# A state-space and attention layer on one core: units of matmuls in half rows, three to three rounds

## The chip, the cores and the metric

One core of a Trainium2 chip runs the whole program as one launch. Its engines are TensorE (matrix products, into the PSUM memory), VectorE, ScalarE, GpSimd and SyncE (which issues DMAs). Each follows its own list of instructions in order, and they wait for one another through semaphores. The metric is the device time of a run in microseconds (us); lower is better.

## The reference

The input is x of 8 sequences x 512 tokens x 256 channels, in fp32. It is layer-normalised to xn, and three results are added to x:

```
u = conv1d(xn @ W_in + b_in, 4 taps, one filter for each of 512 channels) + conv_b
h = tanh(A) h + u_t * Bp ;  ys = Cp . h + Dp * u_t          (a scan over tokens, state of 16)
x += silu(ys) @ W_out + b_out
q, k, v = xn @ W_qkv + b_qkv                                 (16 heads of 16)
x += softmax(q k^T / 4) v                                    (512 x 512 for each head)
gate = softmax(xn @ W_gate + b_gate); the two largest kept as combine weights
x += sum over 8 experts of combine_e * (xn @ W_e + b_e)
```

## The kernel before

**Tiling.** A batch is one sequence: 512 tokens, four blocks of 128 rows. Most products need near-fp32 accuracy and are made of three: an operand is split into a rounded high part and the rest, and high x high, low x high and high x low are accumulated in one PSUM bank (`three`, L460). A *unit* is such a group with a bank of its own. Its kinds: T transposes xn (2 a batch), V makes values and gate logits (4), Q makes queries and keys (4), Z is the scan as a product with a Toeplitz matrix of its response (2), Y is the input projection on Z's result (4), M is half a pair of experts for one token block (16), O is the output projection (4), C transposes the combine weights (1), X transposes the row maxima (4), P transposes attention results (4), B and D belong to the start. M, Q and Y are 6 matmuls of 128 rows x 512 columns. Units share three PSUM banks, `FB`.

**Rounds.** The program is written as rounds t = 0, 1, ... (STEPS = 256, plus LAG = 11 and a few). Attention runs on pairs of heads of a group of four. In a round TensorE first does `score(t)` (L581): two matmuls of 48 rows each, one on rows 0 to 47, one on rows 64 to 111, into the two banks of `SB`. VectorE takes the row maxima of SB (`largest`, L1044), and the next score waits for it (`s_mx`). Then comes `turned(t - LAG)` (L595), the transposed scores less the maximum, again two matmuls of 50 rows, into the two banks of `TB`. ScalarE's exp (L827) turns TB into Pt, and the next turned score waits for that exp (`s_ex`). In every fourth round `values` (L612) multiplies 2 x 2 tiles of Pt with V, in four column groups, into `OB`. After these come the units of the round.

**Planner.** `plan` (L53) decides at build time in which round each unit goes. It spends TensorE time evenly by a table of costs (COST), knows of VectorE's load (VECTOR), takes units in the order of WANTED (32 b plus an offset in rounds) once `soonest` allows, and puts none in a round with values. A unit is read by ScalarE, and where it has a low part by VectorE, in its own round (`late`, all but the last unit) or at the start of the next (`early`, the last one). Reading M is two scaled copies into `mt`, a ring of NM = 4 buffers, and GpSimd adds each to `acc` (`grow`, L1114). The conv of Y is four taps on VectorE (`conv`, L884), one in each of the four rounds after the reading; then ScalarE's tanh, VectorE's gating product (L1082), ScalarE's high part yh and GpSimd's low part yl.

**Other queues.** SyncE copies query and key rows into the stacks `qst` and `kst` (rings of three groups, 12 DMAs a group, `half_stack`, L420) five rounds before a group's first score, once the turned scores that read the ring's old group are done, and the maxima's rows (`max_row`, L1260) after each X.

## Time and profile before

| | us |
|---|---|
| runs shown, median (lowest, highest) | 787.6 (786.55, 788.08) |
| span of the profiled execution | 784.0 |
| TensorE busy | 756.4 |
| VectorE busy | 582.2 |
| ScalarE busy | 534.5 |
| GpSimd busy | 389.7 |

The page gives the span, from the first to the last instruction of the execution that was profiled, as that execution's time; the runs of the table are others, without the profiler. Busy is the time in which an engine had at least one instruction in work. Matmuls are pipelined and the ends of their records are modelled, so that records overlap, and one has to look at the distances between their starts. The granted TensorE clock is full from the second slice of the span on.

### The profile page before, as it was taken

To read this page: it belongs to the slowest core of one execution; us is meant where nothing else is said; L and a number is where in the kernel's file an instruction comes from. 1 tells how busy PE (TensorE), PEld (TensorE's weight loads), DVE (VectorE), ACT (ScalarE), POOL (GpSimd) and SP (SyncE) were. 2 spreads that over 40 slices of the span, in tenths; PEclk is the share of its full clock that TensorE was granted. 3 is DMA by queue.
4 is the path that set the end of the run, shared out by engine and by line. 5 is a ranking of instruction groups with operands and counts; after the bars stand their busy time and mean duration, and the time that the engine had idled before them with its cause. 6 is when DMAs were issued, how large, how long until landed. Compare 5 with 4: busy or idle time off the path is not lost.

```text
span 784.0 us, 13236 instructions
## 1 busy us (share of the span) xinstructions
PE 756.4 (96%) x4408; PEld 455.7 (58%) x4408; DVE 582.2 (74%) x846; ACT 534.5 (68%) x926; POOL 389.7 (50%) x522
## 2 busy tenths in 40 slices
PE   9889999999999999999999999989999999999996
PEld 7566656566555665556555565556655565555553
DVE  6679785977679765897759877698767987568920
ACT  5546775676666766777667776667666776767775
POOL 8347482456344834455346373445444473435654
PEclk9979999999999999999999999999999999999999
DMA  8302111122110221102111121103111111112000
GB/s 272 68 8 66 46 24 30 30 69 69 35 29 22 69 69 41 42 15 82 42 42 42 42 86 32 39 23 96 42 42 43 42 49 41 46 39 69 22 2 27
DMA packets 32465, 39.09 MB, mean 50 GB/s; under 512 B 8513, under 2 KB 18535, under 8 KB 32398
## 3 DMA queue, kind: packets, MB, share of 16 engines
q1 hardware_dynamic: 31418, 37.29, 18.1%
q10 hardware_dynamic: 980, 0.96, 0.6%
q8 instruction: 35, 0.57, 0.3%
q14 instruction: 32, 0.26, 0.1%
HBM read 8.74 MB, written 4.19 MB: 17 GB/s over the span
## 4 chain that ended last, share of the span: by engine, by line
PE 80%; DVE 13%; issue 3%; POOL 2%; ACT 2%; DMA 0%; ACTq 0%; DVEq 0%; POOLq 0%
PE PS L464 38%; PE PS L624 13%; PE SB L591 12%; PE TB L608 7%; PE PS L521 4%; DVE mx L1049 4%; DVE xn L1026 2%; DVE ys L900 2%; PE PS L480 2%; DVE qkl L926 1%; POOL acc L1118 1%; PE PS L631 1%; DVE xl L932 1%; PE PS L476 1%; PE PS L555 1%
## 5 line engine op out<-in xcount | busy, mean ns | idle before, releaser
L1049 DVE TENSOR_REDUCE mx<-SB 128x2 f32<-128x1024 f32 x256 | 312.6, 1221 | 145.2 <-PE SB L591 144.3
L1118 POOL TENSOR_TENSOR acc<-acc,mt 128x256 f32<-128x256 f32 x320 | 252.7, 798 | 244.4 <-ACT mt L674 181.7
L827 ACT ACTIVATE Pt<-TB 128x1024 f32<-128x1024 f32 x251 | 257.5, 1026 | 58.1 <-PE TB L608 54.5
L674 ACT ACTIVATE mt<-PS,cpad 128x256 f32<-128x256 f32 x256 | 107.4, 470 | 58.5 <-PE PS L464 56.5
L591 PE MATMUL SB<-kst,qst 48*128 48x512 f32 x512 | 128.2, 497 | 12.1 <-DVE mx L1049 11.7
L624 PE MATMUL PS<-Pt,V 128*17 128x512 f32 x1024 | 122.3, 595 | 0.0
L591 PEld LDWEIGHTS SB<-kst,qst 48*128 48x128 f32 x512 | 47.8, 183 | 122.4 <-DVE mx L1049 70.3
L464 PE MATMUL PS<-weh,xTh 128*128 128x512 f32 x256 | 109.8, 429 | 1.9 <-DVE xTl L913 1.2
L608 PE MATMUL TB<-qst,kst 50*128 50x512 f32 x502 | 101.3, 399 | 1.3 <-ACT Pt L827 1.3
L464 PE MATMUL PS<-wel,xTh 128*128 128x512 f32 x256 | 100.9, 394 | 0.0
L464 PE MATMUL PS<-weh,xTl 128*128 128x512 f32 x256 | 100.7, 393 | 0.0
L900 DVE SCALAR_TENSOR_TENSOR ys<-uc,cwc,ys 128x511 f32<-128x511 f32 (+2 forms) x96 | 87.4, 910 | 0.0
L464 PEld LDWEIGHTS PS<-weh,xTh 128*128 128x128 f32 x256 | 48.4, 189 | 29.5 <-issue 15.3
L624 PEld LDWEIGHTS PS<-Pt,V 128*17 128x17 f32 x1024 | 23.5, 96 | 63.0 <-issue 62.6
L1243 POOL TENSOR_TENSOR yl<-th,yh 128x512 fp32r<-128x512 f32 x32 | 42.9, 1339 | 31.6 <-ACT yh L760 31.6
L464 PEld LDWEIGHTS PS<-wel,xTh 128*128 128x128 f32 x256 | 48.1, 188 | 11.1
L464 PEld LDWEIGHTS PS<-weh,xTl 128*128 128x128 f32 x256 | 48.4, 189 | 7.0
L608 PEld LDWEIGHTS TB<-qst,kst 50*128 50x128 f32 x502 | 47.7, 186 | 5.9 <-ACT Pt L827 5.5
L1127 POOL TENSOR_TENSOR acc<-acc,at 128x256 f32<-128x256 f32 x31 | 23.1, 747 | 55.4 <-DVE at L960 54.6
L464 PE MATMUL PS<-wouth,yh 128*128 128x256 f32 x128 | 37.3, 292 | 0.3 <-DVE xl L932 0.3
L464 PE MATMUL PS<-woutl,yh 128*128 128x256 f32 x128 | 35.9, 280 | 0.0
L464 PE MATMUL PS<-wouth,yl 128*128 128x256 f32 x128 | 35.9, 280 | 0.0
(162 smaller groups left out, 1138.9 us busy)
## 6 DMA issues: line engine op xcount, KB each, us to landing
qst<-qkh SPq DMA_DIRECT2D x124, 64.0 KB, 2.3
kst<-qkh SPq DMA_DIRECT2D x124, 64.0 KB, 2.3
out<-acc SPq DMA_DIRECT2D x8, 512.0 KB, 2.8
qst<-qkl SPq DMA_DIRECT2D x62, 64.0 KB, 2.2
kst<-qkl SPq DMA_DIRECT2D x62, 64.0 KB, 2.3
acc<-in_x SPq DMA_DIRECT2D x7, 512.0 KB, 3.9
Bt<-in_wexp SPq DMA_DIRECT2D x2, 512.0 KB, 8.0
raw<-in_wexp SPq DMA_DIRECT2D x2, 512.0 KB, 8.5
```

The costliest lines, as they stand in the source:

```text
L464: ins = e.matmul(P, u, v, start=(start and k == 0), stop=(stop and k == n - 1))
L521: ins = e.matmul(P[:, lo:lo + n], p[:, c, fs], q[:, r:r + n], start=(k == 0), stop=(k == 11))
L591: ins = e.matmul(SB[:, h, :], qst[rows, g % 3, jj, 128 * a:128 * a + 128], kst[rows, g % 3, jj, :], start=True, stop=True)
L608: ins = e.matmul(turned_bank(t)[:, h, :], kst[rows, g % 3, jj, 128 * a:128 * a + 128], qst[rows, g % 3, jj, :], start=True, stop=True)
L624: ins = e.matmul(OB[32 * j:32 * j + 17, :], V[:, g // 4 % 2, a, 4 * (g % 4) + j, :], Pt[:, (2 * m + j % 2) % NP, j // 2, :], start=(a == 0 ...
L674: return e.activation(mt[:, item % NM, :], P, ACT.Copy, scale=scale)
L827: e.activation(Pt[:, T % NP, :, :], turned_bank(T)[:, :, :], ACT.Exp, scale=0.25).then_inc(s_ex, 1)
L900: ins = e.scalar_tensor_tensor(out=y[:, s:512], in0=v[:, 0:512 - s], scalar=cwc[:, d, 3 - s:4 - s], in1=y[:, s:512], op0=ALU.mult, op1=ALU ...
L1049: e.tensor_reduce(mx[:, g % 2, 0:2, 4 * jj + a], SB[:, :, :], AX.X, ALU.max).then_inc(s_mx, 1)
L1118: e.tensor_tensor(v, v, mt[:, item % NM, :], ALU.add).then_inc(s_mt, 1)
L1127: e.tensor_tensor(v, v, at[:, :].rearrange("p (a c) -> p a c", a=4), ALU.add).then_inc(s_ad, 1)
L1243: e.tensor_tensor(yl[:, d, :], th[:, :], F(yh[:, d, :]), ALU.subtract).then_inc(s_yl, 1)
```

## The change

Rounds are grouped by four. The numbers of rows in a matmul, and where a unit goes, change as follows.

- LAG is 12, so that values fall in rounds with t % 4 = 0.
- M, Q and Y (24 a batch) go into rounds t % 4 = 1, 2, 3, in threes a, b, c. `side_by_side` does half of each of two units' products: 6 pairs of matmuls, one of the pair on rows 0 to 63 of its operands, the other on rows 64 to 127. The pairs are (a, c), (b, a), (c, b), so each unit has its lower rows in one round and its upper rows in another, accumulated in its bank.
- Rounds with t % 4 = 0 hold values, then X, P or up to two of T, C, V, which now use the halves of TB as banks 3 and 4 (after the exp of the same round; the next turned score waits until they are read), then one of Z, O, V, B at full height in one of the three banks. X is a matmul with the identity on 16 columns of maxima instead of a transpose of 72.
- Units a are read in round 3, b and c in the next round 0, the whole unit in the next round 1.
- The planner places each tap, gating product and high part of Y by VectorE's load (`room`), at most 2.3 us a round by its own figures, 3.2 where t % 4 = 0. VectorE does a second tap of a round and the gating after its unit readings. Layer norm goes one piece a round over eight rounds; the gate's steps are spread over eleven rounds (`GATE` has a second column of rounds).
- zh and zl get tensors of their own, and both matmuls of a score and of a turned score increment the semaphore. The two Z are read one by one.
- The first eight rounds hold up to two units each.

The products themselves are collected by a new generator, `products(u)`, which yields what `three` was called with before; a unit at full height goes through it in a loop (`in_one`).

```diff
-LAG = 11
+LAG = 12
 END = STEPS + LAG + 5
 FREE = STEPS - LAG + 1
 NP = 5
 NM = 4
+CYCLE = 8
...
+WANTED = {("T", i): -60 for i in range(2)}
 WANTED.update({("V", i): -30 for i in range(4)})
-WANTED.update({("Z", i): -20 for i in range(2)})
-WANTED.update({("Q", i): -30 for i in range(4)})
-WANTED.update({("Y", i): 4 * i - 8 for i in range(4)})
+WANTED.update({("Z", i): -52 for i in range(2)})
+WANTED.update({("Q", i): -30 + 8 * (i // 2) for i in range(4)})
+WANTED.update({("Y", i): 4 * i - 20 for i in range(4)})
-WANTED.update({("O", i): i // 2 * 8 + 6 + i % 2 * 2 for i in range(4)})
+WANTED.update({("O", i): i // 2 * 8 + i % 2 * 2 for i in range(4)})
...
+READ = {"T": 0.7, "V": 0.17, "Q": 0.75, "Z": 0.7, "P": 0.7, "X": 0.28}
+
+LN = {b: max(32 * b - 29, 0) for b in range(1, NB)}
...
+GATE_US = {"m": 0.2, "z": 0.2, "r": 0.2, "x0": 0.2, "q0": 0.4, "y0": 0.2, "k0": 0.45, "d": 0.2, "x1": 0.2, "q1": 0.4,
+           "y1": 0.2, "k1": 0.45, "l": 0.5}
...
+    vector = {t: 1.25 * (0 <= t < STEPS) for t in range(-2, END + 60)}
+    for g in range(NG):
+        vector[8 * g + 8] += READ["X"]
+        vector[8 * g + LAG + 12] += READ["P"]
+    for b in range(1, NB):
+        for k in range(4):
+            vector[LN[b] + k] += 0.6
+            vector[LN[b] + 5 + k] += 0.6
...
+    def most(t):
+
+        if t < 16:
+            return 2.6
+        return (3.2 if t % 4 == 0 else 2.3) - 1.0 * (t >= STEPS) * (t % 4 == 0)
+
+    def room(us, t):
+
+        while vector[t] + us > most(t):
+            t += 1
+        vector[t] += us
+        return t
...
+            first = max(r, taps[n - 1][3], gating[n - 2] + 1 if n >= 2 else 0) if n else max(r, 8)
+            taps[n] = []
+            for s in range(4):
+                first = room(0.93, first)
+                taps[n].append(first)
+            gating[n] = room(0.82, max(first + 2, yhi[n - 1] + 2 if n else 0))
+            yhi[n] = gating[n] + 1
...
+        elif t % 4 == 0:
+            room_tb = 2 if t % 8 == 4 or t > STEPS + LAG else 0
+            while room_tb:
+                u = take(lambda u: u[0] in "TCV" and soonest(*u) <= t and (u[0] != "T" or room_tb == 2 - u[2]))
+                if u is None:
+                    break
+                whole[t].append(u)
+                put(u, t, t)
+                room_tb -= 1
+            left = sum(u[0] in "QYM" for u in todo)
+            slots = 3 * ((STEPS + LAG - t) // 4)
+            u = take(lambda u: u[0] in "ZOVB" and soonest(*u) <= t)
+            if u is None and left > slots:
+                u = take(lambda u: u[0] == "M" and soonest(*u) <= t)
+            if u is not None:
+                whole[t].append(u)
+                put(u, t, t + 1)
+            if t < STEPS + LAG - 3:
+                three = []
+                for late in (1, 1, 2):
+                    u = take(lambda u: u[0] in "QYM" and soonest(*u) <= t + late
+                             and not (u[0] == "Y" and any(v[0] == "Y" for v in three)))
+                    if u is not None:
+                        three.append(u)
+                if len(three) == 3:
+                    a, c, b = three
+                    if c[0] == "Q" and a[0] != "Q":
+                        a, c = c, a
+                    sides[t + 1], sides[t + 2], sides[t + 3] = (a, c), (b, a), (c, b)
+                    for u, n in ((a, 1), (c, 1), (b, 2)):
+                        at[u] = t + n
+                    put(a, t + 2, t + 3)
+                    put(b, t + 3, t + 4)
+                    put(c, t + 3, t + 4)
...
+            if CYCLE <= t < STEPS + LAG and done[u] == read[u]:
+                give(u, (4 if u[0] == "P" or u[0] != "X" and n else 3,), t)
+            else:
+                give(u, range(3), t + n / 8)
+        for u in sides.get(t, ()):
+            if u not in unit:
+                give(u, range(3), done[u] + 0.9)
...
+TURNED_AFTER = {}
+for _u in UNIT.values():
+    if _u.bank > 2:
+        TURNED_AFTER.setdefault(max(_u.t + 1 - LAG, 0), []).append(_u)
...
+        FB = [P[:, :] for P in PS[1:4]] + [TB[:, h, :] for h in range(2)]
...
-                e.wait_ge(s_ST, 8 * (g - 2))
+                e.wait_ge(s_ST, 16 * (g - 2))
...
+            def side_by_side(low, up):
+
+                for u in (low, up):
+                    if u not in begun:
+                        bank_there(u)
+                        operands_there(u)
+                if low in begun:
+                    e.wait_ge(s_high, begun[low])
+                if up in begun:
+                    e.wait_ge(s_low, begun[up])
+                for k, ((o, v, w, _), (p, a, b, _)) in enumerate(zip(products(low), products(up))):
+                    below = e.matmul(o, v[0:64], w[0:64], start=(k == 0 and low not in begun), stop=(k == 5 and low in begun),
+                                     skip_group_check=True)
+                    above = e.matmul(p, a[64:128], b[64:128], start=(k == 0 and up not in begun),
+                                     stop=(k == 5 and up in begun), skip_group_check=True)
+                if low in begun:
+                    below.then_inc(s_full[low.bank], 1)
+                else:
+                    below.then_inc(s_low, 1)
+                    begun[low] = firsts[0] = firsts[0] + 1
+                if up in begun:
+                    above.then_inc(s_full[up.bank], 1)
+                else:
+                    above.then_inc(s_high, 1)
+                    begun[up] = firsts[1] = firsts[1] + 1
+
+            def bank_there(u):
+                if u.before is not None:
+                    e.wait_ge(*bank_read(u.before))
+                elif u.bank > 2:
+                    e.wait_ge(s_kp, 1)
+                    e.wait_ge(s_kv, 17)
+                if u.bank > 2 and u.t >= LAG:
+                    e.wait_ge(s_ex, u.t - LAG + 1)
...
+                for u in TURNED_AFTER.get(t, ()):
+                    e.wait_ge(*bank_read(u))
...
                 for h in range(2):
                     rows = slice(64 * h, 64 * h + 50)
-                    ins = e.matmul(turned_bank(t)[:, h, :], kst[rows, g % 3, jj, 128 * a:128 * a + 128], qst[rows, g % 3, jj, :],
-                                   start=True, stop=True)
-                ins.then_inc(s_ST, 1)
+                    e.matmul(turned_bank(t)[:, h, :], kst[rows, g % 3, jj, 128 * a:128 * a + 128], qst[rows, g % 3, jj, :],
+                             start=True, stop=True).then_inc(s_ST, 1)
 
...
                 for m in values_at(t):
                     values(m)
+                if t in SIDES:
+                    side_by_side(*SIDES[t])
                 for u in AT[t]:
                     unit(u)
...
-                for s in (3, 2, 1, 0):
-                    for b, d in y_read(t - s - 1):
-                        conv(b, d, s)
                 for u in early(t):
                     if u.kind != "D":
                         unit(u)
-                for b, d in y_read(t - 5):
-                    e.wait_ge(s_th, 4 * b + d + 1)
-                    e.scalar_tensor_tensor(out=th[:, :], in0=th[:, :], scalar=1.0, in1=ys[:, d % 2, :], op0=ALU.add,
-                                           op1=ALU.mult).then_inc(s_y, 1)
+                taps = taps_at(t)
+                for b, d, k in taps[0:1]:
+                    conv(b, d, k)
                 for b, name in gate_at(t, "DVE"):
                     gate(b, name)
                 for b in range(1, NB):
-                    if t - LN[b] in (0, 1):
-                        layer_norm(b, 2 * (t - LN[b]))
-                        layer_norm(b, 2 * (t - LN[b]) + 1)
-                    elif 3 <= t - LN[b] < 5:
-                        layer_norm(b, 2 * (t - LN[b]) - 1)
-                        layer_norm(b, 2 * (t - LN[b]))
+                    k = t - LN[b]
+                    if 0 <= k < 4 or 5 <= k < 9:
+                        layer_norm(b, k)
                 for u in late(t):
                     unit(u)
                     if t == -1 and (u.kind, u.i) == ("T", 1):
                         split(W_VG)
+                for b, d, k in taps[1:]:
+                    conv(b, d, k)
+                for b, d in gating_at(t):
+                    e.wait_ge(s_th, 4 * b + d + 1)
+                    e.scalar_tensor_tensor(out=th[:, :], in0=th[:, :], scalar=1.0, in1=ys[:, d % 2, :], op0=ALU.add,
+                                           op1=ALU.mult).then_inc(s_y, 1)
                 at_start(t)
```

## Rows read from the trace of the kernel before

**Rows 1.** The head of the page

```profile
span 784.0 us, 13236 instructions
```

**Rows 2.** A window over rounds 8 to 255; timeline rows of its outer scores

```profile
54.70:751.60 696.90, 683.08 (x4004) 406.95 (x4003) 540.84 (x760) 487.14 (x832) 343.92 (x455) 1.00 0.18 46
...
54.68 0.50 PE L591 MATMUL SB<-kst,qst 48*128 48x512 f32 x2
...
751.58 0.50 PE L591 MATMUL SB<-kst,qst 48*128 48x512 f32 x2
```

**Rows 3.** Timeline of TensorE: start, duration, engine, line, output<-input, count

```profile
402.32 0.40 PE L464 MATMUL PS<-weh,xTl 128*128 128x512 f32 x1
402.56 0.40 PE L464 MATMUL PS<-wel,xTh 128*128 128x512 f32 x1
402.89 0.50 PE L591 MATMUL SB<-kst,qst 48*128 48x512 f32 x2
403.22 0.40 PE L608 MATMUL TB<-qst,kst 50*128 50x512 f32 x2
403.55 0.50 PE L464 MATMUL PS<-xh,winh 128*128 128x512 f32 x1
403.89 0.40 PE L464 MATMUL PS<-xh,winl 128*128 128x512 f32 x1
```

**Rows 4.** The same stretch, timeline of TensorE's weight loads

```profile
402.89 0.19 PEld L591 LDWEIGHTS SB<-kst,qst 48*128 48x128 f32 x2 [0.37 <-issue]
402.99 0.19 PEld L608 LDWEIGHTS TB<-qst,kst 50*128 50x128 f32 x2
403.55 0.19 PEld L464 LDWEIGHTS PS<-xh,winh 128*128 128x128 f32 x1 [0.37 <-ACT mt L674]
403.66 0.19 PEld L464 LDWEIGHTS PS<-xh,winl 128*128 128x128 f32 x1
```

**Rows 5.** Timeline of TensorE in a round with values, and the score after it

```profile
405.80 1.91 PE L624 MATMUL PS<-Pt,V 128*17 128x512 f32 x16
407.64 0.50 PE L591 MATMUL SB<-kst,qst 48*128 48x512 f32 x2
```

**Rows 6.** Timeline of a round without a long unit

```profile
679.87 0.49 PE L591 MATMUL SB<-kst,qst 48*128 48x512 f32 x2
...
680.41 1.23 DVE L1049 TENSOR_REDUCE mx<-SB 128x2 f32<-128x1024 f32 x1 [1.01 <-PE SB L591]
...
681.69 0.50 PE L591 MATMUL SB<-kst,qst 48*128 48x512 f32 x2 [0.53 <-DVE mx L1049]
```

**Rows 7.** Timeline of VectorE

```profile
415.25 1.21 DVE L900 SCALAR_TENSOR_TENSOR ys<-uc,cwc,ys 128x510 f32<-128x510 f32 x1
416.38 1.21 DVE L1049 TENSOR_REDUCE mx<-SB 128x2 f32<-128x1024 f32 x1
417.52 0.73 DVE L900 SCALAR_TENSOR_TENSOR ys<-uc,cwc,ys 128x509 f32<-128x509 f32 x1
418.18 0.41 DVE L1013 BATCH_NORM_STATS2 st<-acc 128x6 f32<-128x256 f32 x1
```

**Rows 8.** Timeline of ScalarE

```profile
438.43 0.84 ACT L674 ACTIVATE mt<-PS,cpad 128x256 f32<-128x256 f32 x2
439.16 1.03 ACT L827 ACTIVATE Pt<-TB 128x1024 f32<-128x1024 f32 x1
```

**Rows 9.** Groups by shape, then the page's group of taps: count | busy, mean ns

```profile
L913 DVE TENSOR_TENSOR xTl<-PS,xTh 128x512 fp32r<-128x512 f32 x16 | 10.3, 675 | 0.0
...
L1118 POOL TENSOR_TENSOR acc<-acc,mt 128x256 f32<-128x256 f32 x320 | 252.7, 798 | 244.4 <-ACT mt L674 181.7 <-ACT mt L673 42.6 <-POOL acc L1118 0.4
...
L900 DVE SCALAR_TENSOR_TENSOR ys<-uc,cwc,ys 128x511 f32<-128x511 f32 (+2 forms) x96 | 87.4, 910 | 0.0
```

**Rows 10.** Timeline of SyncE: issues of a stack; the page: issue, us to landing

```profile
462.93 1.29 SPq L437 DMA_DIRECT2D qst<-qkh  x2
...
qst<-qkh SPq DMA_DIRECT2D x124, 64.0 KB, 2.3
```

More of the change, by code:

```diff
@@ new lines, in plan @@
+def plan():
+    whole = {t: [] for t in range(-2, END + 1)}
+    sides = {}
+    at, done, read = {}, {}, {}
+    taps, gating, yhi = {}, {}, {}
+    xh = {0: -1}
+    todo = sorted([(k, b, i) for b in range(NB) for k, i in WANTED if b == 0 or k != "B"],
+                  key=lambda u: 32 * u[1] + WANTED[u[0], u[2]])
+    vector = {t: 1.25 * (0 <= t < STEPS) for t in range(-2, END + 60)}
[15 more added lines that the diff above has]
+        return t
@@ L93, in soonest @@
+            return max(t, after(("B", 0, 3), 1) if b == 0 else after(("O", b - 1, i // 2 * 2 + 1), 0))
         if kind in "CM":
[L94 to L109 removed]
+            late = {name: g[2 if b == 0 else 3] for name, g in ((g[0], g) for g in GATE)}
@@ new lines, in take @@
+    def take(test):
+        k = next((k for k, u in enumerate(todo) if test(u)), None)
+        return None if k is None else todo.pop(k)
+    for t, row in FIRST.items():
+        for k, (kind, i) in enumerate(row):
+            u = (kind, 0, i)
+            if u in todo:
+                todo.remove(u)
+            whole[t].append(u)
+            put(u, t, t + (k == len(row) - 1))
+    for t in range(2, END):
+        g = normal_at(t)
+        if g is not None:
+            u = ("P", g // 4, g)
+            whole[t].append(u)
+            put(u, t, t)
@@ new lines, in plan @@
+        assert b == 0 or done["C", b - 1, 0] < done["V", b, 3] + 9
+        assert b < 2 or done["M", b - 2, 15] < done["V", b, 3] + 9
+        assert b == 0 or xh[b - 1] + 4 < LN[b] + 5 and done["T", b - 1, 1] < LN[b] + 5
+    order = sorted(done, key=lambda u: (read[u], done[u] == read[u]))
+    ends = {t: [] for t in whole}
+    for u in order:
+        ends[read[u]].append(u)
+    item = {u: 2 * n for n, u in enumerate(u for u in order if u[0] in "MO")}
+    uses, frees, held, busy = [0] * 5, [0] * 5, [None] * 5, [-9] * 5
@@ new lines, in plan, with give @@
+    unit = {}
+    def give(key, banks, n):
+        kind, b, i = key
+        bank = min(banks, key=lambda j: busy[j])
+        busy[bank] = n
+        uses[bank] += 1
+        frees[bank] += kind not in "MO"
+        unit[key] = Unit(kind, b, i, at[key], done[key], read[key], bank, uses[bank], frees[bank], item.get(key), held[bank])
+        held[bank] = unit[key]
+    for t, row in whole.items():
+        for n, u in enumerate(row):
+            if CYCLE <= t < STEPS + LAG and done[u] == read[u]:
[5 more added lines that the diff above has]
+                give(u, range(3), done[u] + 0.9)
@@ new lines, in plan @@
+    return ({t: [unit[u] for u in row] for t, row in whole.items()},
+            {t: [unit[u] for u in two] for t, two in sides.items()},
+            {t: [unit[u] for u in row] for t, row in ends.items()}, taps, gating, yhi, xh)
+AT, SIDES, READS, TAPS, GATING, YHI, XH = plan()
+UNIT = {(u.kind, u.b, u.i): u for row in READS.values() for u in row}
+TURNED_AFTER = {}
+for _u in UNIT.values():
+    if _u.bank > 2:
+        TURNED_AFTER.setdefault(max(_u.t + 1 - LAG, 0), []).append(_u)
+KRYLOV = {("T", 1): (1, 2), ("D", 0): (3,), ("D", 1): (4,), ("D", 2): (5,), ("D", 3): (6,)}
```

391 lines of the change are left out of this document (189 added, 202 removed), and 7 rows, old and new, of the table GATE.

## The prediction, made before the changed kernel ran

> **What bounds the kernel now.** The page gives a span of 784.0 us [rows 1]. The median of the runs shown is 787.6 us, 3.6 above that span; I make the sum on the span and carry the difference over. A window over the steady part, from the score of round 8 (54.68) to that of round 255 (751.58), has 247 rounds in 696.9 us [rows 2], so four rounds (a cycle, since the P V products come every fourth round) take 696.9 / 61.75 = 11.29 us. TensorE is busy 683.1 of it, VectorE 540.8, ScalarE 487.1, GpSimd 343.9.
>
> A "busy" TensorE says little by itself, so next comes its timeline, matmul by matmul [rows 3]. Inside an expert unit, matmuls of 512 columns start 0.23 apart. From the unit's last to the score it is 0.33, from score to turned score 0.33, from there to the next unit 0.33, and from that unit's first matmul to its second 0.34. The weight loads explain it [rows 4]: the score's load starts together with its matmul's record (402.89), not under the matmul before it, and so does the unit's (403.55); the turned score's two loads start at 402.99, under the score's stream, and its matmuls follow 0.23 later. So each change between half-height pairs (rows 0 to 63 beside 64 to 127) and full height costs about 0.10 of emptying and 0.10 of bare load, 0.21 in all. A round has two: 0.41.
>
> Both matmuls of a score or turned score start together and take one slot of 0.23 before the next starts. That is the evidence that two half-height matmuls run side by side at the price of one.
>
> **What the change removes.** Streamed columns stay the same: a unit of 6 full-height matmuls becomes 12 of half height, in pairs with another unit's. Three units in three rounds are 18 pairs x 0.23, as 18 full matmuls were. What goes is the change of mode. Before, a cycle has 8 changes (2 x 4; in the round with values, turned to values and values to score). After, rounds t%4 = 1, 2, 3 are half height throughout, and round 0 has three: turned to values, values to whole unit, whole unit to the next score. Five fewer x 0.21 = 1.03 us a cycle. TensorE's own need falls from 11.29 to 10.26.
>
> Cross-check from below: a paired round is 8 pairs x 0.232 = 1.86, three with one bare load 5.68 [rows 3, 4]. Round 0 is score and turned 0.56, values 1.84 [rows 5], on average 2.1 of whole units and transposes (per batch Z 4.0, O 6.4, V 3.2, T, C, P and X 3.3 from their column counts at 0.23 per 512) and 0.1 of emptying: 4.6. The sum is 10.28.
>
> **What it makes late next.** Now a paired round is so short that others can end last. Three waits appear.
>
> (a) VectorE's chain. Row by row in [rows 6]: a score recorded at 679.87 lets the row maximum start at 680.41 (0.54), which runs 1.23, and the next score comes at 681.69: 1.82 a round with nothing else on VectorE, just under 1.86. VectorE's records overlap: maximum to next instruction is 1.14, and a tap is followed after 0.66, or after 1.13 in its slow form (415.25) [rows 7]; mean duration 0.91 less 0.08 of overlap gives 0.83 a tap. The three paired rounds then last at least 0.54 + 1.14 + o1 + 1.14 + o2 + 1.23 + 0.05 = 4.10 + o1 + o2, where o1 and o2 is VectorE's other work of rounds 1 and 2 (that of round 3 falls into the long round 0). It costs when o1 + o2 is over 1.58. I walked the new planner through one batch of 32 rounds: it fills each paired round to its limit of 2.3 less 1.25, that is one tap a round (or layer norm at 0.55, a Q or Z split at 0.6 to 0.7, and what the planner's table GATE_US says of the gate). o1 + o2 comes to 1.93, 2.11, 1.68, 1.66, 2.26, 2.13, 0.7, 0 for the eight cycles, so 0.35 + 0.53 + 0.10 + 0.08 + 0.68 + 0.55 = 2.3 us a batch.
>
> (b) ScalarE in round 0. Units b and c of a trio both end in round 3 and are read in round 0 ahead of the exp: two M are four copies, 0.73 a pair, then exp at 1.03 [rows 8]. They start about 0.2 into the round, so the exp ends at 0.2 + 1.48 + 1.03 = 2.71. The transposes of round 0 now go to the halves of TB and wait for this exp; TensorE is there at 0.56 + 1.84 = 2.40. That is a stall of 0.36 when b and c are two M, less with a Q or Y, none where VectorE's chain delayed the round; with a tanh ahead 0.48. Over a batch I count 1.5 us.
>
> (c) The two T of a batch in TB (t = 12 of 32). The next turned score must wait until ScalarE has cast and VectorE has subtracted both (0.68 for each subtraction [rows 9]; 0.6 for each cast is an estimate from the exp of twice its columns [rows 8]), and this batch puts a tap behind them. T's are written from 2.73 to 3.6, subtractions end near 5.3, the tap at 6.0, so the next maximum starts 1.8 later than TensorE alone would allow: 1.8 us a batch.
>
> Together 5.6 us a batch, 0.70 a cycle. The last batch has no next one to prepare, about 0.2; averaged with it, 0.64. The waits of before that vanish are about 0.1 and I leave them.
>
> **Edits priced at nothing.** Zh and zl of their own only loosen a wait. Two Z in separate rounds, each read by itself, cost the same work. X as a plain matmul with 16 columns: still 0.06. The taps after the units' reads: the total is unchanged, its place is in (a). For the stacks of group g SP issues 12 DMAs at 0.65 (7.7 us) and the last lands 2.3 later, 10 us after the turned score of round 8g-5 has freed the ring [rows 10]; with LAG 12 instead of 11 this comes a round later, but round 3, a round 0 and three paired rounds are 1.9 + 4.0 + 5.7 = 11.6 at least, less 0.7 to the release. It fits by about 1 us; without that cover each us by which it is missed is paid once a group, 30 us over the kernel. More rows of SP (max rows, 4 issues) stand ahead of it, but are done in round 0. GpSimd adds each half M at 0.80 [rows 9]: 8 in a cycle of 11 are 6.4, plus yl and xl; its four mt buffers are freed in time unless it lags.
>
> LAG + 1 adds one round to the end, without a score: 1.1 to 2.0, taken as 1.5. The first eight rounds keep their work and their start-up waits, taken at 0 (bounds -3 to +3, one unit's worth of two matmul groups either way).
>
> One rule speaks against it: the page "TensorE: Matmul & The Clock Gate" of the Trainium skill (The cost: per-tile semaphore tail) gives about 26 ns for each further increment, and the change adds one to each score and turned score. By it some 30 ns would stand before each maximum and exp. No run here shows it yet; the sum without it stands.
>
> **The sum.** 11.29 - 1.03 + 0.64 = 10.90 us a cycle; x 61.75 this is 24 us less; + 1.5: 22.5 less, 765. Counted from below (65 us for rounds 8 to 31, six batches at 45.4 + 36.8 + 5.6 = 87.8, the last 78) the cycles take 670 us instead of 699.5, which gives 759.5. I take the middle, 762.
>
> **Rivals.**
> 1. *The waits hide.* The planner leaves VectorE's work where round 0 covers it, and neighbours' slack absorbs (b) and (c). Then only 1.03 x 61.75 = 63.6 is left of the terms: 725.5; with half the waits, 745. For it: a fifth of VectorE's time is free [rows 2]. Against: that slack sits in round 0.
> 2. *VectorE and ScalarE chain at full duration* (the other side). If the overlap of records is lost and more taps are slow, because GpSimd works beside them, the chain is 4.27 + o1 + o2 with taps at 0.91 and more: 4.6 us a batch for (a), 2.9 for (b) (four copies at 0.47), 2.0 for (c), 1.19 a cycle, 1.07 averaged: 11.33, +2.5 + 1.5 gives 792. It decides from 1.03 us of waits a cycle, 0.39 above mine. For it: tap means of 0.91 lie between 0.66 and 1.13 [rows 7, 9]. Against: the overlaps in rows 7 and 8.
> 3. *GpSimd's ring.* ScalarE's third and fourth copy in round 0 wait for an addition that a yl held up (over 1 us, an estimate from 0.80 for half its columns [rows 9]); each cycle with one loses 0.9 and the exp, hence the transposes, come late. Half the cycles: 0.45 x 61.75 = 28, 790. Against: GpSimd is idle half the time [rows 2].
> 4. *The pairs don't overlap in a long run.* Each load of a half would wait for the matmul of its own half: 18 bare loads x 0.107 = 1.9 us a cycle, 119 us, 881. Rows 3 and 4 speak against it: the turned score's loads start under the score's matmuls on the same rows. But they show one pair behind one pair, not 48 pairs in a row, and none that accumulates. The Trainium skill, page "TensorE: Matmul & The Clock Gate" (The mechanism), says that a load overlaps matmuls in flight only when the row group differs, which would be this rival; by the full-height loads of rows 4 the trace disagrees.
>
> **Chances.** Forecast (748 to 778) 0.51; rival 1, 0.17; rival 2, 0.17; rival 3, 0.10; rival 4, 0.05. What a measurement of this kernel can tell from no change is about 0.2%, 786.0 to 789.2. A quarter of rivals 2 and 3 still ends below that band, so faster is 0.51 + 0.17 + 0.06 = 0.74; of the rest 0.05 within it, 0.21 slower. Leaving out the lower half of rival 1 and the worst of 2 to 4, the range is 738 to 796; the likeliest case's own is 748 to 778.
>
> **What would show it.** In the changed trace, paired matmuls of two units starting together, a pair every 0.23, and no 0.33 step between turned score and the pairs (else rival 4). Cycles of 10.8 to 11.0 us. TensorE's waits for VectorE's maximum at the scores of rounds 2, 3 and 0 in cycles with taps; waits of the transposes for the exp of the same round, near 0.3; one long wait at t = 13 of each batch for xTl. ScalarE's copies waiting for GpSimd would be rival 3, taps near 1.2 throughout rival 2. Scores waiting for stack DMAs would show that the LAG sentence was wrong.

## The result and the profile after

| | before | after |
|---|---|---|
| runs, median (lowest, highest), us | 787.84 (786.55, 789.42) | 766.25 (764.93, 767.8) |
| ratio of the medians, 95% interval | | 0.9731 [0.9707, 0.9756] |
| span of the profiled execution | 784.0 | 764.9 |

The change makes the kernel 21.6 us faster; 762 was forecast, with 738 to 796 as its range. Head of the page after, with the first row of its busy times (busy, share of the span, instructions), to set beside [rows 1]:

```profile
span 764.9 us, 15809 instructions
...
PE 723.7 (95%) x5568; PEld 487.4 (64%) x5568; DVE 559.9 (73%) x845; ACT 531.8 (70%) x926; POOL 389.8 (51%) x522
```

The window from the score of round 8 to that of round 255, as in [rows 2]. Its ends are the starts of the two scores' weight loads, and so it is with all lengths of rounds and batches below; in the changed kernel a score's matmul starts 0.12 behind its load where pairs stand before it (round 255's at 732.11). The row gives (length; busy and instructions of TensorE, weight loads, VectorE, ScalarE, GpSimd; granted clock; DMA share; GB/s):

```profile
58.10:731.99 673.89, 654.93 (x5155) 441.87 (x5157) 515.63 (x759) 486.05 (x837) 347.16 (x457) 0.99 0.19 47
```

So these 247 rounds take 673.9 us, against 696.9, and a cycle 673.89 / 61.75 = 10.91 (10.90 was forecast). The start up to round 8 is 3.4 us longer (58.1 against 54.7) and the end after round 255 0.5 longer (764.9 - 732.0 against 784.0 - 751.6): -23.0 + 3.4 + 0.5 = -19.1, the difference of the spans.

**A paired round.** TensorE and its loads in round 138 from its score on (start, duration; a load's line is PEld). L765 is the score, L783 the turned score, L677 and L679 the lower and upper halves of a pair:

```profile
417.01 0.19 PEld L765 LDWEIGHTS SB<-kst,qst 48*128 48x128 f32 x2
417.13 0.41 PE L765 MATMUL SB<-kst,qst 48*128 48x512 f32 x2
...
417.36 0.41 PE L783 MATMUL TB<-qst,kst 50*128 50x512 f32 x2
...
417.60 0.40 PE L679 MATMUL PS<-xTh,wqkh 64*128 64x512 f32 x1
417.60 0.19 PEld L679 LDWEIGHTS PS<-xTh,wqkl 64*128 64x128 f32 x1
...
417.61 0.39 PE L677 MATMUL PS<-weh,xTh 64*128 64x512 f32 x1
417.61 0.19 PEld L677 LDWEIGHTS PS<-weh,xTl 64*128 64x128 f32 x1
...
417.84 0.39 PE L679 MATMUL PS<-xTh,wqkl 64*128 64x512 f32 x1
...
417.84 0.40 PE L677 MATMUL PS<-weh,xTl 64*128 64x512 f32 x1
...
418.07 0.39 PE L679 MATMUL PS<-xTl,wqkh 64*128 64x512 f32 x1
```

Score to turned score 0.23, to the first pair 0.24, pair to pair 0.24 and 0.23: the steps of 0.33 of [rows 3] are gone. Two things are to be seen. The halves of two units start together and take one slot. And the loads for the pair of 417.84 start at 417.60, with the matmuls of the pair before them on the same rows. A round without a wait lasts 1.85 to 1.86.

**Round 0.** TensorE and ScalarE in round 136, t = 8 of its batch, from the values (L798) on. L1004 is the exp, L711 is P, L706 is X, L663 the whole unit; L880 and L851 read the units that ended in round 3:

```profile
410.23 0.69 ACT L880 ACTIVATE qkh<-PS,bq 128x512 fp32r<-128x512 f32 x1 [0.38 <-PE PS L679]
...
410.64 1.91 PE L798 MATMUL PS<-Pt,V 128*17 128x512 f32 x16
410.82 0.83 ACT L851 ACTIVATE mt<-PS,cpad 128x256 f32<-128x256 f32 x2
...
411.54 1.03 ACT L1004 ACTIVATE Pt<-TB 128x1024 f32<-128x1024 f32 x1
...
412.67 0.63 PE L711 MATMUL TB<-ident,ot 128*128 128x128 f32 x4
413.22 0.11 PEld L706 LDWEIGHTS TB<-ident,mx 128*16 128x16 f32 x2 [0.17 <-issue]
413.22 0.39 PE L706 MATMUL TB<-ident,mx 128*16 128x128 f32 x2
...
413.54 0.19 PEld L663 LDWEIGHTS PS<-wouth,yh 128*128 128x128 f32 x1 [0.21 <-issue]
413.55 0.39 PE L663 MATMUL PS<-wouth,yh 128*128 128x256 f32 x1
```

Values take 1.84 [rows 5], so TensorE is free near 412.5; the exp ends at 412.57 and P starts at 412.67. That is term (b), small here: one of the two reads is a Q. From P's first matmul to the whole unit's it is 0.88, and two loads in it stand bare, before X and after it. What X and these two loads take is a cost that the forecast put at 0.06.

**Averages.** The distances between scores, averaged over the five batches 2 to 6 of every trace, give for the kernel after 87.6 us a batch (87.8 was counted): 41.9 in the eight rounds 0 and 45.7 in the 24 paired ones. The sums below compare with these.

**The wait at the T's, and that at t = 26.** VectorE and the score's load, first in round 141 (t = 13), then in rounds 153 to 155 (t = 25 to 27):

```profile
425.33 0.68 DVE L1090 TENSOR_TENSOR xTl<-TB,xTh 128x512 fp32r<-128x512 f32 x1
...
425.93 0.92 DVE L1077 SCALAR_TENSOR_TENSOR ys<-uc,cwc,ys 128x511 f32<-128x511 f32 x1
...
426.77 1.21 DVE L1222 TENSOR_REDUCE mx<-SB 128x2 f32<-128x1024 f32 x1
...
428.04 0.19 PEld L765 LDWEIGHTS SB<-kst,qst 48*128 48x128 f32 x2 [0.42 <-DVE mx L1222]
...
460.12 0.68 DVE L1107 TENSOR_TENSOR zl<-PS,zh 128x512 fp32r<-128x512 f32 x1
...
460.72 0.68 DVE L1266 SCALAR_TENSOR_TENSOR th<-th,ys 128x512 f32<-128x512 f32 x1
...
461.32 1.22 DVE L1222 TENSOR_REDUCE mx<-SB 128x2 f32<-128x1024 f32 x1
...
462.59 0.18 PEld L765 LDWEIGHTS SB<-kst,qst 48*128 48x128 f32 x2 [0.50 <-DVE mx L1222]
```

In the first, the tap behind the second T's subtraction makes the maximum late; the round lasts 2.17, that is 0.32 over a free one, not 1.8. In the second, round 25 has Z's subtraction and a gating product behind its maximum, 1.2 us together; the next score is 0.5 late. It is the largest single loss in a paired round.

**The start.** Round 4, VectorE, GpSimd and TensorE, and the same operation in the trace before:

```profile
36.77 2.34 POOL L1339 TENSOR_TENSOR wel<-Bt,weh 128x1024 fp32r<-128x1024 f32 x1
...
36.95 2.83 DVE L1205 TENSOR_TENSOR Rl<-ys,Rh 128x640 fp32r<-128x640 f32 x1
...
39.93 0.76 PE L663 MATMUL PS<-Rh,xh 128*128 128x512 f32 x1 [3.19 <-DVE Rl L1205]
```

```profile
35.77 0.79 DVE L1032 TENSOR_TENSOR Rl<-ys,Rh 128x640 fp32r<-128x640 f32 x1
...
36.62 2.37 POOL L1168 TENSOR_TENSOR wel<-Bt,weh 128x1024 fp32r<-128x1024 f32 x1
```

The first Z waits 3.2 us for an operation that took 0.79 in the trace before, where the wait was 0.6. In the kernel after it begins 0.18 behind a GpSimd subtraction and ends 0.67 behind that one's end; before, it was through when GpSimd began that subtraction (a short GpSimd product had begun 0.16 after it). All the runs below are like the kernel after in this (2.83 or 2.84, each begun 0.18 behind `wel`). No run moves one of the two alone, so that GpSimd's work is the cause is likely and not shown.

### The profile page after: what moved, and what is told of

The parts are those of the page before. It is cut to its first block, busy times and chain, and to the rows that moved or that the text cites. A ratio compares the mean times of both kernels' runs of the same rounds, so it can differ in the third digit from the quotient of the medians.

```text
span 764.9 us, 15809 instructions
## 1 busy us (share of the span) xinstructions
PE 723.7 (95%) x5568; PEld 487.4 (64%) x5568; DVE 559.9 (73%) x845; ACT 531.8 (70%) x926; POOL 389.8 (51%) x522
## 4 chain that ended last, share of the span: by engine, by line
PE 85%; DVE 7%; issue 4%; ACT 4%; DMA 1%; ACTq 0%; SPq 0%; POOL 0%; DVEq 0%; POOLq 0%
PE PS L677 20%; PE PS L798 14%; PE PS L663 13%; PE PS L679 12%; PE SB L765 9%; PE TB L783 7%; DVE mx L1222 3%; PE TB L711 3%; PE TB L663 2%; ACT Pt L1004 1%; PE TB L706 1%; PE PS L805 1%; ACT mt L851 1%; PE TB L718 1%; PE PS L584 1%
## 5 line engine op out<-in xcount | busy, mean ns | idle before, releaser
L1004 ACT ACTIVATE Pt<-TB 128x1024 f32<-128x1024 f32 x250 | 258.1, 1032 | 53.9 <-PE TB L783 49.7
L798 PE MATMUL PS<-Pt,V 128*17 128x512 f32 x1024 | 123.7, 601 | 0.0
L765 PE MATMUL SB<-kst,qst 48*128 48x512 f32 x512 | 114.7, 437 | 7.8 <-DVE mx L1222 6.9
L851 ACT ACTIVATE mt<-PS,cpad 128x256 f32<-128x256 f32 x256 | 103.8, 478 | 17.2 <-PE PS L679 15.7
L783 PE MATMUL TB<-qst,kst 50*128 50x512 f32 x500 | 103.8, 404 | 2.1 <-DVE xTl L1090 1.2
L677 PE MATMUL PS<-weh,xTh 64*128 64x512 f32 x256 | 102.8, 401 | 0.0
L679 PE MATMUL PS<-weh,xTh 64*128 64x512 f32 x256 | 102.1, 399 | 0.0
L679 PE MATMUL PS<-wel,xTh 64*128 64x512 f32 x256 | 101.2, 395 | 0.0
L679 PE MATMUL PS<-weh,xTl 64*128 64x512 f32 x256 | 100.9, 394 | 0.0
L677 PE MATMUL PS<-weh,xTl 64*128 64x512 f32 x256 | 100.7, 393 | 0.0
L677 PE MATMUL PS<-wel,xTh 64*128 64x512 f32 x256 | 100.6, 393 | 0.0
L765 PEld LDWEIGHTS SB<-kst,qst 48*128 48x128 f32 x512 | 48.4, 185 | 51.1 <-DVE mx L1222 29.0
L1077 DVE SCALAR_TENSOR_TENSOR ys<-uc,cwc,ys 128x511 f32<-128x511 f32 (+2 forms) x96 | 75.0, 781 | 0.0
L798 PEld LDWEIGHTS PS<-Pt,V 128*17 128x17 f32 x1024 | 23.6, 97 | 60.4 <-issue 58.6
L677 PEld LDWEIGHTS PS<-weh,xTh 64*128 64x128 f32 x256 | 47.7, 186 | 14.9 <-DVE zl L1107 3.9
L783 PEld LDWEIGHTS TB<-qst,kst 50*128 50x128 f32 x500 | 49.3, 187 | 7.7 <-issue 2.1
L677 PEld LDWEIGHTS PS<-wel,xTh 64*128 64x128 f32 x256 | 47.7, 186 | 6.7
L677 PEld LDWEIGHTS PS<-weh,xTl 64*128 64x128 f32 x256 | 48.1, 188 | 4.6
L679 PEld LDWEIGHTS PS<-wel,xTh 64*128 64x128 f32 x256 | 47.8, 187 | 3.4
```

The source lines that it names most:

```text
L677: below = e.matmul(o, v[0:64], w[0:64], start=(k == 0 and low not in begun), stop=(k == 5 and low in begun), skip_group_check=True)
L679: above = e.matmul(p, a[64:128], b[64:128], start=(k == 0 and up not in begun), stop=(k == 5 and up in begun), skip_group_check=True)
L765: e.matmul(SB[:, h, :], qst[rows, g % 3, jj, 128 * a:128 * a + 128], kst[rows, g % 3, jj, :], start=True, stop=True).then_inc(s_S, 1)
L783: e.matmul(turned_bank(t)[:, h, :], kst[rows, g % 3, jj, 128 * a:128 * a + 128], qst[rows, g % 3, jj, :], start=True, stop=True).then_inc( ...
L798: ins = e.matmul(OB[32 * j:32 * j + 17, :], V[:, g // 4 % 2, a, 4 * (g % 4) + j, :], Pt[:, (2 * m + j % 2) % NP, j // 2, :], start=(a == 0 ...
L851: return e.activation(mt[:, item % NM, :], P, ACT.Copy, scale=scale)
```

## The experiments

The theory after the two traces: the saving of 1.03 us a cycle is there whole, and what is missing of it is lost in round 0, at X and at the exp. Its rivals: the missing part is VectorE's chain, the forecast's largest term (a), or the pairs themselves bring less than that. Each diff is against the kernel after the change; each ratio is to the kernel before on the same chip, whose medians there were 786.71 (e1 to e4) and 787.52 us (e5 to e8).

**e1: X as the transpose of 72 columns that it was**, with the padding of `mx` set to zero at the start.

```diff
-        mx = sb("mx", [128, 2, 2, 8])
+        mx = sb("mx", [128, 2, 9, 8])
...
-                    ins = e.matmul(P[0:16, 0:128], mx[:, i % 2, :, :].rearrange("p h c -> p (h c)"), ident[:, :],
-                                   start=True, stop=True)
+                    if i == 0:
+                        e.wait_ge(s_init, 5)
+                    ins = e.transpose(P[0:72, 0:128], mx[:, i % 2, :, :].rearrange("p h c -> p (h c)"), ident[:, :])
```

> X again as a transpose of 72 columns of maxima (56 of them zero), as before the change, everything else as changed. Theory: 16 columns put TensorE in another column mode, and the trace after shows 0.20 us between P and X, 0.12 for X's own two passes, 0.20 from X to the whole unit and 0.22 to its second matmul, 0.75 from the last P to the second matmul of the unit; with X at 72 columns this should be about 0.40, so 0.35 x 32 = 11 us less than the changed kernel: 755. Rival: the time is hidden under what round 0 waits for anyway (the reading of TB before the next turned score): no change, 766.

Measured: 754.67 us (753.32 to 756.48), ratio 0.9592 [0.9567, 0.9617]: 11.6 under the change, as expected. (Differences to the change are those of the medians; the kernel before was 1.1 us lower beside e1 to e4 than beside the change, so they are good to 1 or 2 us.) The timeline of a P, an X (L708) and the whole unit behind it:

```profile
404.64 0.63 PE L712 MATMUL TB<-ident,ot 128*128 128x128 f32 x4
405.00 0.12 PEld L708 LDWEIGHTS TB<-ident,mx 128*72 128x72 f32 x1
405.11 0.27 PE L708 MATMUL TB<-ident,mx 128*72 128x128 f32 x1
...
405.14 0.37 PE L663 MATMUL PS<-wouth,yh 128*128 128x256 f32 x1
```

From P to the whole unit 0.50 instead of 0.88, and X's load starts before P's last matmul is through. 0.38 x 32 X is 12 us. The run doesn't tell how much of it is the switch to 16 columns and back and how much X's second pass (x2 in the row of after), since the edit changes both; nor which of the two makes the loads before and after X bare.

**e2: the exp ahead of the second reading.** In round 0 of the kernel after, ScalarE reads b and c and then does the exp; here it reads one, does the exp, reads the other.

```diff
-                for u in early(t):
+                T = t - LAG
+                ahead = 1 if t % 4 == 0 and 0 <= T < STEPS else 9
+                for u in early(t)[:ahead]:
...
+                for u in early(t)[ahead:]:
+                    unit(u)
```

> In rounds with t % 4 = 0 ScalarE does the exp after the first of the two trio units it reads, not after both. Theory: in these rounds the transposes in TB wait for the exp, which ends 2.85 us after the score while TensorE is free at 2.57 or earlier; the waits add up to 2.35 us a batch in the trace after (0.66, 0.19, 0.19, 0.42, 0.35, 0.12, 0.42). With the exp from 1.1 to 2.2 they vanish: 2.35 x 7.5 = 17 us less, 749. Rival: the wait only moves, to the bank of the unit read last or to the low parts on VectorE: under 4 us less, 762 or more.

Measured: 748.88 us (747.18 to 751.02), ratio 0.9525 [0.9491, 0.9558]: 17.4 under the change. Round 136 again:

```profile
397.66 0.69 ACT L880 ACTIVATE qkh<-PS,bq 128x512 fp32r<-128x512 f32 x1 [0.36 <-PE PS L679]
...
398.08 1.91 PE L798 MATMUL PS<-Pt,V 128*17 128x512 f32 x16
398.25 1.02 ACT L1005 ACTIVATE Pt<-TB 128x1024 f32<-128x1024 f32 x1
...
399.15 0.84 ACT L851 ACTIVATE mt<-PS,cpad 128x256 f32<-128x256 f32 x2
...
399.92 0.66 PE L711 MATMUL TB<-ident,ot 128*128 128x128 f32 x4
```

The exp ends at 399.27, and P starts 1.84 behind the values' start: it waits for nothing. The rounds 0 of a batch fall from 41.9 to 39.7 and the paired ones stay at 45.7, so (b) was 2.2 us a batch. The whole trace gains a little more than that, because its rounds 8 to 31 take 62.0 us instead of 67.0, and (b) is only some 1.6 of these 5: from 60 to 80 us the granted clock is 0.92 in this trace and 0.69 in that of the kernel after.

**e3: the same plan at full height.** Each paired round runs the six matmuls of one unit on 128 rows in place of six pairs of half rows (a in round 1, b in 2, c in 3); planner, banks, readings, taps and LAG are the change's.

```diff
...
-                for k, ((o, v, w, _), (p, a, b, _)) in enumerate(zip(products(low), products(up))):
-                    below = e.matmul(o, v[0:64], w[0:64], ...
...
-                    above = e.matmul(p, a[64:128], b[64:128], ...
...
+                bank_there(low)
+                operands_there(low)
+                in_one(low).then_inc(s_full[low.bank], 1)
```

> The changed plan, orders and banks, but each unit of a trio at full height in one round (a in round 1, b in round 2, c in round 3) instead of two half heights side by side. Theory: the whole gain is the change of mode. Now 9 changes a cycle instead of 3: 6 x 0.21 = 1.26 us x 62 cycles = 78 us more, 844; a little less (836) where a wait in round 0 is absorbed. Rival: the gain came from the planner and the spread VectorE work, and half rows only break even: within 5 us of the changed kernel. Second rival, pairs of half rows themselves stream worse than full rows: less than 60 us more.

Measured: 809.43 us (808.83 to 809.69), ratio 1.0284 [1.0255, 1.0314]: 43 above the change, where 70 to 78 was expected. Under 60 was to be the sign of the second rival, that pairs stream worse than full rows; but a pair takes 0.23 to 0.24, as a full matmul does, and what is missing is in the rounds 0, as follows. A paired round of it, now with the steps of before:

```profile
413.93 0.50 PE L745 MATMUL SB<-kst,qst 48*128 48x512 f32 x2
414.26 0.40 PE L763 MATMUL TB<-qst,kst 50*128 50x512 f32 x2
414.59 0.50 PE L663 MATMUL PS<-weh,xTh 128*128 128x512 f32 x1
414.93 0.40 PE L663 MATMUL PS<-weh,xTl 128*128 128x512 f32 x1
...
416.19 0.50 PE L745 MATMUL SB<-kst,qst 48*128 48x512 f32 x2
```

416.19 - 413.93 = 2.26, against 1.86: 0.40 for two changes of mode, as priced. The paired rounds of a batch take 54.1 instead of 45.7, but the rounds 0 take 39.5 instead of 41.9: in longer rounds ScalarE is on time, and the wait for the exp is gone. P, T, C and V start 1.84 behind the values' start but for 0.06 us a batch, against 2.4 in the trace after. If so, half rows are worth more once that wait is gone from both. e8 below asks this.

**e4: one increment for each score and turned score**, as before the change; thresholds to match.

```diff
-                    e.matmul(SB[:, h, :], ...).then_inc(s_S, 1)
+                    ins = e.matmul(SB[:, h, :], ...)
+                ins.then_inc(s_S, 1)
...
-                e.wait_ge(s_S, 2 * t + 2)
+                e.wait_ge(s_S, t + 1)
```

> Score and turned score increment their semaphores once, on the second matmul, as before the change. Theory: a second increment costs next to nothing: 766, within 1 us. Rival, by the page "TensorE: Matmul & The Clock Gate" of the Trainium skill (The cost: per-tile semaphore tail), about 26 ns each. In sentences of its own, as it hangs on that page: one stands before each maximum and each exp, and on the 10 or so of 32 rounds in which one of these ends last this would be 0.03 x 80 = 2 us less, and 14 us less if it counted in all.

Measured: 767.54 us (766.18 to 770.01), ratio 0.9756 [0.973, 0.9782], against 0.9731 of the change: no gain. The medians don't show the second increment, but the traces do, where VectorE or ScalarE waits for TensorE: over rounds 64 to 223 the maximum starts 0.564 behind its score in the kernel after and 0.537 in e4 (medians; 0.541 before), the exp 0.461 and 0.436 behind its turned score. By the Trainium skill's page "TensorE: Matmul & The Clock Gate" (The cost: per-tile semaphore tail) a further increment costs about 26 ns; these 27 and 25 agree. It is too little, and too seldom last, to move the time.

**e5: e1 and e2 together.**

> Both edits that gained: X with 72 columns, and the exp between the two trio units. Theory: they remove different things (bare loads and changes of mode around X; waits for the exp), so they add: 766.3 - 11.6 - 17.4 = 737. Rival: an earlier X only waits longer for the reading of TB, and the shorter round 0 lets VectorE end last: 743 or more.

Measured: 736.68 us (736.01 to 737.02), ratio 0.9356 [0.9342, 0.9371]. The two gains add (11.6 + 17.4 = 29.0, measured 29.6), so they are separate stalls in series; a batch is 1.3 shorter in e1, 2.2 in e2 and 3.2 here. This version beats both kernels, by 51 and by 30 us. Its window from round 8 to 255, and its score group's idle time with what ended it:

```profile
57.08:702.53 645.45, 638.30 (x5124) 439.11 (x5124) 514.93 (x759) 485.60 (x837) 349.12 (x457) 1.00 0.20 49
```

```profile
L766 PE MATMUL SB<-kst,qst 48*128 48x512 f32 x512 | 114.9, 439 | 10.2 <-DVE mx L1226 7.1 <-DMA kst<-qkl 2.6
```

A cycle is 10.45; the row shows scores that wait for a stack's DMA, 2.6 us in all, up to 0.9 at t = 24. Such waits are 0.2 us in all in the kernel after and 1.2 in e1: the cover of about 1 us that the forecast gave those DMAs was just used up by the change, and the faster versions pay.

**e6: taps in four consecutive rounds**, without the planner's limit (`room`) on taps and gating; LAG, pairs and readings as in the change.

```diff
-                first = room(0.93, first)
-                taps[n].append(first)
-            gating[n] = room(0.82, max(first + 2, yhi[n - 1] + 2 if n else 0))
+                taps[n].append(first + s)
+                vector[first + s] += 0.93
+            first += 3
+            gating[n] = max(first + 2, yhi[n - 1] + 2 if n else 0)
+            vector[gating[n]] += 0.82
```

> The changed kernel with the taps of a Y in the four rounds from its reading on, whatever VectorE's load (as before the change), the gating two rounds after the last; units find other rounds by this. Theory: VectorE's chain grows: four paired rounds a batch hold a tap beside layer norm or gate steps, and T's two subtractions at t = 12 have no whole unit behind them, so the next turned score waits 1.5 to 1.8 us there instead of 0.3: about 2.2 us a batch more, 16 us, 782. Rival: VectorE has slack enough, the spreading brings nothing: within 3 us of 766.

Measured: 793.06 us (792.54 to 794.53), ratio 1.0071 [1.0053, 1.0089]: 27 above the change, where 16 was expected, and 5.5 above the kernel before. A batch takes 92.6, the paired rounds 51.4 of it. TensorE at the scores of rounds 134 to 136, which end rounds 133 to 135, and the T round 141 with VectorE:

```profile
419.42 0.49 PE L767 MATMUL SB<-kst,qst 48*128 48x512 f32 x2 [0.27 <-DVE mx L1224]
...
422.08 0.50 PE L767 MATMUL SB<-kst,qst 48*128 48x512 f32 x2 [0.53 <-DVE mx L1224]
...
425.38 0.50 PE L767 MATMUL SB<-kst,qst 48*128 48x512 f32 x2 [1.18 <-DVE mx L1224]
...
439.69 0.50 PE L767 MATMUL SB<-kst,qst 48*128 48x512 f32 x2
...
439.98 1.29 DVE L1092 TENSOR_TENSOR xTl<-TB,xTh 128x512 fp32r<-128x512 f32 x2
...
441.41 0.50 PE L785 MATMUL TB<-qst,kst 50*128 50x512 f32 x2 [1.22 <-DVE xTl L1092]
```

Both waits of the forecast are here: VectorE's chain, 2.0 us of waits at three scores in succession, and the T wait, a turned score 1.72 behind its score instead of 0.33. A batch has 51.4 - 44.5 = 6.9 us of them (44.5 is 24 free rounds), some 1.5 at the T's and 5.4 on the chain. It is more than was expected. Without the limit the units find other rounds too (here no whole unit follows the T's), so the run prices the levelling as a whole and not a tap's place alone: it is worth more than the change as a whole gains.

**e7: one tap of four.** The conv's taps 1 to 3 are left out (a `return` where they begin, and the thresholds of those that wait for taps to match), so the output isn't the reference's.

```diff
-                    e.wait_ge(s_cv, 4 * n + s)
+                    return
```

> The changed kernel without taps 1 to 3 of the convolution (only tap 0 is computed), which takes 96 instructions and 75 us of records off VectorE. Theory from the trace after: VectorE ends last by 0.5 us in round 26 of each batch and by 0.1 in three others; gone, this is 0.9 x 7.5 = 7 us less, 759. The prediction's term (a) of 2.3 us a batch would be 18 us less, 748. Rival, VectorE is off the path altogether: 766.

Measured: 764.38 us (762.86 to 764.9), ratio 0.9706 [0.9688, 0.9724]: 1.9 under the change, where 7 was expected. A batch takes 87.3 instead of 87.6; the T wait at t = 13 is gone, the wait at t = 26 stays at its 0.5, which the expectation had put down to the taps: Z's subtraction and the gating product, which this run keeps, make it. So 96 operations of 0.78 us, 75 us of VectorE, stand almost wholly beside other work, where the planner has put them.

**e8: e3 with both edits of e5.**

> e3 (trio units at full height, one to a round) with the two edits of e5. Theory: in the changed kernel the paired rounds of 1.86 us leave ScalarE behind, and some 17 us of what half rows give is lost to waits for the exp in round 0, while at full height (2.25) ScalarE keeps up and the edit of the exp gives little there. So here X gives its 12 and the exp 0 to 3: 809.4 - 12 - 2 = 795, and half rows are worth 795 - 737 = 58 us with the fixes, against 43 without. Rival: the two kernels gain the same from both edits: 809.4 - 29 = 780, half rows worth 43 again.

Measured: 799.15 us (799.0 to 800.67), ratio 1.0155 [1.0138, 1.0173]. Against e5 at 736.68, half rows are worth 62.5 us; without the two edits they were worth 43.2. At full height the two edits together bring 10.3, about what X alone brings in pairs, and in pairs they bring 29.6; the rounds 0 of a batch fall from 39.5 to 37.8 from e3 to this run, and by 1.7 from the change to e1. So in pairs a part of the saving was given back in round 0, at the exp. How large it is depends on where one looks: 19 us by the medians, but a batch takes 93.6 in e3, 87.6 in the change, 92.1 here and 84.4 in e5, so that half rows are worth 6.0 a batch without the edits and 7.6 with them, and over the 7.7 batches of the window that is 46 and 59, 13 apart. The other 6 lie in the start, where the four traces were granted different clocks from 60 to 80 us (0.88, 0.69, 0.70, 0.93).

## Why the prediction was right, step by step

- **The mechanism held.** Three rounds in a row at half height without a change of mode, 0.23 a pair, 1.86 a round. Rival 4 (pairs that don't overlap) is refuted by the fence of the paired round: loads run under matmuls on their own rows, also where a pair accumulates and over the 24 pairs of three rounds (the forecast's 48 are their matmuls). The rule of the Trainium skill's page "TensorE: Matmul & The Clock Gate" (The mechanism), by which a load overlaps matmuls in flight only when the row group differs, does not describe this; what the same section says of loads into a background weight buffer, which are pulled ahead, would.
- **The saving of 1.03 us a cycle held.** From e3's paired round a change of mode is 0.20; there are nine in the plan at full height, three in pairs, eight before. 6 x 0.20 x 61.75 = 74 us bounds what pairs can bring; 62.5 was measured. The plan alone has a ninth change, 0.20 x 61.75 = 12 us: e8 stands 11.6 above the kernel before, and its batch takes 92.1 against 90.4. The change saves the five that are left, 1.0 a cycle.
- **Term (a), VectorE's chain, 2.3 us a batch: too large.** The paired rounds of a batch take 45.7, and 24 free ones 24 x 1.855 = 44.5. Of the 1.2 over, 0.3 is the T wait and 0.5 the one at t = 26, so (a) is 0.9 in all, of which the taps are next to nothing (e7). The step that failed is the plan walked: the real one puts whole units, Z and taps some rounds away from where I had them, so that the sums o1 + o2 were those of another plan. With the list that the planner itself gives for batch 4 and the forecast's prices (and 0.6 for a gating product, its record of 0.68 less the overlap), o1 + o2 pass 1.58 in four cycles only (rounds 5 and 6, 13 and 14, 17 and 18, 25 and 26), by 0.17, 0.08, 0.08 and 0.45, some 0.8 together. That is an estimate, near the 0.9 measured: the forecast's formula was fed with the wrong rounds. Nor is this wait new: the page of before has 11.7 us of scores that wait for the maximum, 0.19 a cycle, the page of after 6.9. The forecast left the old waits out at 0.1. The fast form of a tap was also more frequent than the mean of [rows 9] let me assume (781 ns in the page after, 910 before).
- **Term (b), the exp in round 0, 1.5 us a batch: too small.** e2 took away 2.2. The mechanism is as put. In the trace after the transposes come late in seven of the eight rounds 0 of a batch, 2.4 together. The four rounds in which b and c are both M wait 0.37 on average (0.67, 0, 0.37, 0.45), where 0.36 was forecast (the forecast's own 2.71 less 2.40 gives 0.31); the four with a Q or Y still wait 0.9 together. How the hand walk came to 1.5 is not on record.
- **Term (c), the T wait, 1.8: too large.** It is 0.3, since a whole O follows the T's at t = 12 and hides their readings. Where none does (e6) it is 1.5.
- **X "still 0.06": wrong by 0.38 each, 12 us.** The count went by streamed columns and left out the bare loads on either side of X and its second pass. If the loads are bare because of the 16 columns, this was a change of mode of its own, and the sum was built on the price of such changes.
- **Start 0, end + 1.5.** Measured + 3.4, of which 2.6 is the wait for Rl (3.2 against 0.6 before), and + 0.5. Nor is the clock full from the second slice on, as the part on the kernel before has it: the trace before has 0.94 from 19.6 to 39.2 us and 0.80 from 39.2 to 58.8. In the trace after it is low for longer, as this window shows (before it is 1.00 from 55 to 75 us):

```profile
60.00:80.00 20.00, 16.57 (x91) 12.85 (x92) 14.62 (x22) 9.41 (x18) 6.24 (x8) 0.69 0.27 68
```

  0.69 is a mean over stretches at the full level of 2.4 GHz and at the half one, 1.2 GHz. In the 24 us before (36 to 60) TensorE was busy for 15.1, in the trace before for 21.3. Rounds 8 to 31 then take 67.0 us, where 65 was counted. No run was made for it, but the trace of e5, with 0.93 from 60 to 80 us, has 61.4 there, and only some 2.4 of the difference are its two edits.
- **The sum.** By the count from below: 65 + 6 x 87.8 + 78 = 670 was forecast, 67.0 + 526.0 + 80.9 = 673.9 came; what makes the last batch 2.9 longer was not looked into. The 699.5 that this count was set against is in no row. With the 696.9 of [rows 2] it gives 762 and not 759.5, and the middle would have been 764. Within a batch, (a) and (c) were 2.9 too large; (b) and X 2.2 too small. The rest nearly balances: 24 free paired rounds take 44.5 where 45.4 was counted, and e5's rounds 0, without either stall, 38.1 where 36.8 was. Most of both is the choice of the load's start as the mark, which moves 0.12 us a cycle from the paired rounds to round 0; 0.4 a batch stays open. So 87.6 against 87.8 is right partly because errors cancel: the forecast of the total was better than that of its terms.
- **Rivals 1 to 3.** Rival 1 (the waits hide, 725.5 to 745) is what e5 is close to, but only after the two edits. Rival 2's full-duration chain did not come, taps were faster than before. What it feared of taps beside GpSimd is there (the last section has the count), only less often than before. For rival 3, ScalarE's copies that wait for GpSimd, the waits after show none among the large ones. Scores that wait for a stack's DMA, the sign that the sentence on LAG was wrong, make 0.2 us in the kernel after.

## What to carry to other kernels

Count changes of TensorE's tile mode, not columns alone: here each between full and half rows costs about 0.2 us of drain and bare load, and it paid to gather work of one mode in successive rounds. A small helper product can cost as much, as X did. When a stage becomes faster, look at the order in which its results are read: here one exp moved ahead of a reading was worth four fifths of the whole change. A plan that a program computes should be listed by the program before waits are priced on it; the hand-walked one had the right mechanisms in the wrong rounds.

## What the runs showed of the hardware that was not expected

- Accumulating pairs of 64-row matmuls of two units run at 0.23 a pair over 18 pairs in three rounds, the pitch of one 128-row matmul [rows 3], with loads on the same rows hidden.
- X as a matmul with 16 columns of weights, in two passes between matmuls of 128, has a bare load on either side, and together this is 0.38 us more than X as a transpose of 72 columns in one pass.
- A second semaphore increment on a pair of matmuls makes the engine that waits for it start 27 and 25 ns later (0.564 against 0.537 us, 0.461 against 0.436) and is not seen in the time (766.25 against 767.54 us).
- The same VectorE operation on 128 x 640 took 0.79 us in one kernel and 2.83 in the other; the mean of taps 1 to 3 was 781 ns after and 910 before. Both go with GpSimd. Of the 256 taps of the two traces, 62 had no GpSimd instruction beside them, and none of these took over 0.75 us; of the 131 that began while one was running, 89 took over 0.78 (up to 1.59). It is a count from the two traces, not an experiment.
